# One VectorE instruction with a PSUM operand in place of two, in a graph attention kernel on one core

## The reference

```
alpha = a_src[src] + a_dst[dst] (+ a_edge)        # one value per edge and head
alpha = leaky_relu(alpha, 0.2)
m = segment_max(alpha, dst)
ea = exp(alpha - m[dst])
den = segment_sum(ea, dst)
out = segment_sum(xp[src] * ea[:, :, None], dst)  # later divided by den
```

## Time and profile before

| what | value |
|---|---|
| median of 3 runs | 8124.74 us (8120.78 to 8137.6) |
| time of the profiled execution | 8132.4 us |
| its span | 8130.6 us |
| mean granted clock of TensorE | 0.759 |
| DVE busy | 4106.7 us, 51% of the span |
| PE busy | 4968.6 us, 61% |
| POOL busy | 3807.1 us, 47% |
| the two `weigh` instructions of 110 batches | 2283 ns each in g2, 2283 in g3 |

### The profile page before, as it was taken

How to read it: one execution, slowest core, us unless ns; L and a number is a source line. 1 busy time by engine, 2 the same in 40 slices (tenths; PEclk the granted TensorE clock), 3 DMA queues, 4 the chain that set the end, 5 groups by cost and what they waited for, 6 DMA issues and landing times. The chain is left out here.

```text
span 8130.6 us, 99773 instructions
## 1 busy us (share of the span) xinstructions
PE 4968.6 (61%) x21937; PEld 3493.2 (43%) x21938; DVE 4106.7 (51%) x8878; ACT 3148.1 (39%) x9208; POOL 3807.1 (47%) x3656
## 2 busy tenths in 40 slices
PE   1777777777877875555555355655653355555651
PEld 0555555555655663344443233333332233333331
DVE  2344444444444664222222546666667656666668
ACT  1555555555555323333334233333333333333332
POOL 1233333333333102666666046666664266666663
PEclk7888888888888667777777677777776667777775
DMA  5322222222222102434343133333331233333332
GB/s 197 91 50 49 53 52 49 50 54 50 49 55 49 30 18 86 113 111 114 111 113 104 48 112 108 108 109 107 109 109 44 63 105 106 106 105 105 107 104 71
DMA packets 675121, 685.46 MB, mean 84 GB/s; under 512 B 454519, under 2 KB 542809, under 8 KB 672974
## 3 DMA queue, kind: packets, MB, share of 16 engines
q0 software_dynamic: 171984, 482.58, 20.8%
q1 hardware_dynamic: 492941, 188.51, 9.3%
q10 hardware_dynamic: 10016, 12.59, 0.4%
HBM read 625.13 MB, written 65.79 MB: 85 GB/s over the span
## 5 line engine op out<-in xcount | busy, mean ns | idle before, releaser
L913 POOL DMA_INDIRECT c0rows<-rows,c0idx x880 | 832.3, 946 | 1593.8 <-DVE c0prod L1069 1342.3
L1525 POOL DMA_INDIRECT g3rows<-sender_rows,g3idx x880 | 976.9, 1110 | 617.9 <-issue 232.3
L1525 POOL DMA_INDIRECT g2rows<-sender_rows,g2idx x880 | 975.2, 1108 | 571.5 <-issue 229.8
L721 POOL DMA_INDIRECT g1rows<-rows,g1idx x880 | 831.6, 945 | 687.0 <-issue 243.8
L953 ACT ACTIVATE c0selk<-c0sel,c0sh 128x128 f32<-128x128 f32 x3520 | 1063.0, 392 | 3.1 <-PE c0psA L1022 3.1
L754 PE MATMUL g1psA<-g1rows,g1sel 128*128 128x257 f32 x1760 | 606.8, 519 | 554.6 <-issue 421.2
L1022 PEld LDWEIGHTS c0psA<-c0prod,c0selk 128*128 128x128 f32 x5280 | 829.7, 215 | 67.0
L832 DVE TENSOR_TENSOR acc<-acc,g1psA 128x257 f32 x880 | 372.1, 423 | 949.3 <-issue 554.0
L1019 PE MATMUL c0psA<-c0prod,c0selk 128*128 128x256 f32 x1760 | 658.0, 460 | 298.2 <-DVE acc L1084 283.0
L1022 PE MATMUL c0psA<-c0prod,c0selk 128*128 128x128 f32 x5280 | 820.2, 297 | 0.0
L754 PEld LDWEIGHTS g1psA<-g1rows,g1sel 128*128 128x128 f32 x1760 | 462.5, 271 | 685.3 <-issue 550.0
(11 more groups left out here) (412 smaller groups left out, 7901.8 us busy)
## 6 DMA issues: line engine op xcount, KB each, us to landing
g2bc<-dst_rows SPq DMA_DIRECT2D x55, 512.0 KB
g3bc<-dst_rows SPq DMA_DIRECT2D x55, 512.0 KB
g1f<-in_edge_attr SPq DMA_DIRECT2D x83, 320.0 KB
c0rows<-rows,c0idx POOLq DMA_INDIRECT x880
g1rows<-rows,g1idx POOLq DMA_INDIRECT x880
g2rows<-sender_rows,g2idx POOLq DMA_INDIRECT x880
g3rows<-sender_rows,g3idx POOLq DMA_INDIRECT x880
rbf_steps<-prep_extra ACTq DMA_DIRECT2D x7, 1024.0 KB, 5.7
```

The source lines that it names most:

```text
L721: g.indirect_dma_start(rows[b][:, u, 0:D], None, k.table, bass.IndirectOffsetOnAxis(ap=idx[b][:, u:u + 1], axis=0)).then_inc(r_sem[b], 16)
L913: g.indirect_dma_start(rows[b][:, u, :], None, k.table, bass.IndirectOffsetOnAxis(ap=idx[b][:, u:u + 1], axis=0)).then_inc(g_sem[b], 16)
L1525: g.indirect_dma_start(rows[b][:, u, 0:TW], None, k.sender_rows, bass.IndirectOffsetOnAxis(ap=idx[b][:, u:u + 1], axis=0)).then_inc(gas[b] ...
```

## The change

ScalarE computes the exponential twice: once from PSUM into columns 384 to 511 of the same PSUM bank, then once as before into `rows[b]`. VectorE's product takes the weights from PSUM, broadcast over the 32 channels, and handles all 16 steps in one instruction, which adds 2 to `msg` when it ends. TensorE's transpose of `z` into that bank now also waits until that product of the batch before has ended.

```diff
             def turn(t):
                 pe.wait_ge(S["z"], t + 1)
-                reach(pe, S["w"], t)
+                reach(pe, S["msg"], t * 2)
                 nc.tensor.transpose(psT[:, 0:P], z[:, :, :].rearrange("p h u -> p (h u)"), k.ident[:, :]
                                     ).then_inc(S["zt"], 1)
...
+                nc.scalar.activation(psT[:, 3 * P:4 * P], psT[:, P:2 * P], ACT.Exp)
                 nc.scalar.activation(by, psT[:, P:2 * P].rearrange("p (h u) -> p h u", h=H), ACT.Exp
                                      ).then_inc(S["w"], 1)
                 one_hot(t, 0)
...
             def weigh(t, b, i):
                 v.wait_ge(S["w"], t + 1)
-                for half in range(2):
-                    u = slice(half * (U // 2), (half + 1) * (U // 2))
-                    r = rows[b][:, u, 0:TW].rearrange("p u (h c) -> p u h c", c=HW)
-                    nc.vector.tensor_tensor(r[:, :, :, 0:CH], r[:, :, :, 0:CH],
-                                            r[:, :, :, CH:HW].broadcast_to([P, U // 2, H, CH]), ALU.mult
-                                            ).then_inc(S["msg"], 1)
+                weight = psT[:, 3 * P:4 * P].rearrange("p (h u) -> p u h", h=H)
+                r = rows[b][:, :, 0:TW].rearrange("p u (h c) -> p u h c", c=HW)
+                nc.vector.tensor_tensor(r[:, :, :, 0:CH], r[:, :, :, 0:CH],
+                                        weight.unsqueeze(3).broadcast_to([P, U, H, CH]), ALU.mult).then_inc(S["msg"], 2)
```

## The result

| | median | range | runs |
|---|---|---|---|
| before | 8122.76 us | 8120.01 to 8137.6 | 4 |
| after | 8267.51 us | 8264.44 to 8275.23 | 4 |

The changed kernel takes 1.0181 of the time, 95% interval 1.0169 to 1.0194. That is 145 us more; the profiled executions differ by 137.3 us (8132.4 and 8269.69). This holds for the chip of the first measurement. What the runs show of both follows. Ratios are estimated from all runs of a kernel, so they lie up to 0.0006 beside the quotient of two medians; left out are one run of the kernel before on chip 3 (9144.82 us) and one of late_gather_b on chip 4 (9582.89 us), both over 30% above the rest.

The account below looks back on a forecast made before the run. Each interval was taken as weigh, score, products, gather 0 (7.6 us), then 18.6 us tied to gathers. Delays of 167, 6 and 4 us sum to 177: 8309 profiled, less 7.7, gives 8302 us; range 8175 to 8345.

Parts of the forecast that it names:

- the 18.6 us behind gather 0: From gather 0 to the next weigh: a stretch that stays fixed, so a later gather 0 moves the weigh one for one.
- One instruction: VectorE's weigh: one instruction takes 4.41 us where two halves take 4.48, a gain of 0.07 us.
- The operand in PSUM: VectorE's weigh: reading the factor from PSUM adds nothing, as `rescale` broadcasts from PSUM at the plain product's cost.
- The other end: VectorE's weigh: dear PSUM reads, 0.72 ns an element, +2.9 us a batch; as a rival 8620 us, chance 0.05.
- The second exponential: ScalarE before the weigh: 0.3 to 0.5 us more, costing nothing within 1.9 us of cover, at worst 0.4.
- TensorE's start: Product 0 waits for the whole weigh, 2.13 us later; product 3 and gather 0 move by 1.9 us, to about +9.5.
- The wait in `turn`: TensorE's added wait costs nothing, since it has waited for `msg` of the same batch before product 0.
- How many batches: Batches of g2 and g3 that pay the delay: 102 - 14 = 88, by 1.9 us, 167 us.
- The intervals without gathers: Four intervals bound by VectorE, whose `within` waits for the later transpose: 4 x 1.5 = 6 us.
- the shrinking: Sign of a wrong forecast: the stretch from gather 0 to the next weigh shrinks when gather 0 comes later.
- Gathers beside the weigh: GpSimd: back to 0.95 us if VectorE's two SBUF operands hold them; 2.25 us freed, worth nothing behind product 3's wait.
- The rival: Faster: if GpSimd's own queue set gather 0, 2.25 us off 102 intervals, 230 us, so 7895 us; chance 0.04.

Follow-up runs that it names:

- late_gather_b: Kernel before with gather 0 (and so 1 to 3) waiting for product 5 instead of product 3; 6945.07 us, ratio 0.9998 to before.
- experiment 4: On top of experiment 1, each gather waits for its own step's product, where gathers 0 to 3 waited for product 3; 8398.20 us, ratio 1.0148 to before.
- experiment 1: Changed kernel with the weigh in two halves again, PSUM factor and second exponential kept; 8287.15 us, ratio 1.0009 to the kernel before.
- experiment 2: Kernel before with the weigh merged into one instruction, factor still from SBUF, no second exponential; 8394.90 us, ratio 1.0146 to before.
- experiment 3: Kernel before with the second exponential alone, written to PSUM and read by nobody; 8278.39 us, ratio 1.0004 to before.
- guard_rescale: Kernel before with gather 12 waiting for the semaphore of the rescale at the batch's end instead of product 15's; 6944.99 us, ratio 1.0001 to before.

## Why the prediction held on the first chip, and where it did not

*What bounds the kernel.* On chips 1 and 2 as said: gathers, in a way I couldn't name, set 7 us of each interval. The step that read the 18.6 us behind gather 0 as fixed was too strong. They are twelve gathers and mostly 4.6 to 5.4 us behind the last one (experiment 4). With the guards unchanged the two say the same in most batches, and so the forecast came out right: the trace that it was read from and the result are of the same chip. Carried over to chip 3 it has the wrong sign. What holds the other engines stays open.

*One instruction.* 4.41 forecast, 4.411 measured as the mean of 51. Right.

*The operand in PSUM.* No extra cost: 4.48 for two halves with either factor (experiment 1). The other end, 2.9 us a batch, is out. The Trainium skill (VectorE: DVE Perf Modes, "The TRN2 errata") gives a PSUM source a fixed cost 62 cycles higher. An estimate by it is 0.13 us more for the two halves. The rows don't bear it out: 4.48 both ways, and for one instruction 4.411 from PSUM against 4.416 from SBUF (experiment 2).

*The second exponential.* Nothing, as forecast; shown alone by experiment 3. That the one-hot matrices are ready long before product 0 is true of most batches of the changed kernel. With two halves it is not always so: in 17 of the 51 intervals of g2 in experiment 1 product 0 waits for them and starts 0.2 us late.

*TensorE's start.* Product 0 at +4.55 as forecast; the transpose's pass at +7.34 against +7.3, gather 0 at +9.43 against +9.5. The six passes of the first three products cover 3.00 us, as before, so the clock did not come to their help. Experiments 1 and 2 show that this start, and neither operand nor exponential, is the cause on a chip with holds: undone, the ratio is 1.0009; alone, 1.0146. That it works through gather 0, and not through the late products themselves, is argued from the timelines and not shown: no run with gather 0 late alone fell on a chip with holds. Two things speak for it. In experiment 4 nothing but the gathers' guard was changed against experiment 1, and the batch grew by 1.4 us in g2. And where no holds arise, the late products fit into a batch of 20.4 us: in g2 on chip 3 (21.3 in g3), and in the short batch shown below on chip 1.

*The wait in `turn`.* No row of VectorE or TensorE has it as a wait of its own. Nothing, as forecast.

*How many batches.* This term was mis-sized: 88 batches by 1.9 us, 167 us, where the 102 intervals measure 51 x 1.53 and 51 x 1.10, 134 us. In most intervals the delay is 1.8 as forecast (the one shown: 27.95). What the count left out is every sixth batch. There GpSimd stands 1.8 to 1.9 us behind gather 0, in both kernels, and the profile names no reason. In the kernel before 13 of the 16 such batches take 26.4 to 27.5 us. In the changed kernel they are the short ones, 20.4 to 27.3 us: in most of them the weigh comes while the run of gathers still lasts. The batch after each pays with 28.8 to 35.3. One such pair, GpSimd's rows and then VectorE's:

```profile
5082.31 0.95 POOL L1525 DMA_INDIRECT g2rows<-sender_rows,g2idx  x1 [1.86 <-issue]
...
5107.64 0.95 POOL L1525 DMA_INDIRECT g2rows<-sender_rows,g2idx  x1 [6.73 <-PE g2psA L1551]
```

```profile
5070.47 4.41 DVE L1741 TENSOR_TENSOR g2rows<-g2rows,g2psT 128x4096 f32<-128x4096 f32 x1
...
5090.91 4.41 DVE L1741 TENSOR_TENSOR g2rows<-g2rows,g2psT 128x4096 f32<-128x4096 f32 x1
...
5126.20 4.41 DVE L1741 TENSOR_TENSOR g2rows<-g2rows,g2psT 128x4096 f32<-128x4096 f32 x1
```

The first takes 20.44 us, the second 35.29. So the median gather 0 is 1.8 us later in g2 and 1.9 in g3, with 18.6 us behind it as before. In the mean it is 2.4 and 1.8 us later, and the stretch behind it is 0.9 and 0.7 us shorter. That is the shrinking which the prediction named as a sign of being wrong, and it comes for the most part from these pairs. The intervals without gathers grew by 1.0 and not 1.5.

*Gathers beside the weigh.* That VectorE's two SBUF operands hold them was right, on every chip. The rule of the Trainium skill (SBUF — State Buffer, "Who interferes with whom") has VectorE with two SBUF inputs contend with GpSimd instructions that read SBUF. All these runs agree with it if issuing a gather counts as one of them, which the section doesn't say: 0.95 us with one SBUF input, 1.89 to 5.08 with two. The same section of the Trainium skill says that `tensor_tensor` was not seen to stall a DMA. For these gathers the rows show that it does. That this is "worth nothing" was right only under its own condition, that GpSimd waits for product 3 anyway. The rival named the mechanism and the point from which it decides, GpSimd's own queue setting the gathers, and priced it at 2.25 us an interval, 230 us. On the chips without holds that point is passed. The changed kernel gains 194 us on chip 3, 1.8 us an interval in the mean, since the merging takes some back in g3; with the halves kept the gain is 239 us on chip 4, close to that price. Its chance of 0.04 was worked out from one chip's trace, and that could not show that there are chips on which the holds are absent.

## What to carry to other kernels

When work is handed on in parts, the first part's end is what the next engine starts from: one instruction over everything costs the consumer half the producer's time, here 2.1 us for 0.07 saved. A VectorE product with two SBUF operands may stop GpSimd's gathers for as long as the instruction lasts; a PSUM operand avoids it, and it pays as soon as GpSimd's queue is the bound. An edit that you price at nothing because another wait covers it should be priced without the cover too: here the cover was there on some chips and not on others, and the sign of the change with it.

## What the runs showed of the hardware

- The same program takes 17 to 19% longer on two chips (8122.76 and 8278.74 us) than on three others (6941 to 6946). The durations of single instructions are the same (the weigh 4.41, a gather 0.95). What differs is that on the first two semaphore waits of VectorE and ScalarE, and with them TensorE's work, end late while GpSimd issues a run of gathers. VectorE's adds are then 2.82 us apart instead of 0.64, and GpSimd's own wait for product 15 ends late too: gather 12 starts at 5488.04 in the batch shown, though TensorE's last product began before 5478.80. Of the 1180 us between chips 1 and 3, some 750 lie ahead of the first weigh of g2 (it starts at 4778 us on chip 1, and at 4033 in guard_rescale on chip 3), in other layers that gather too; that these have the same holds is not shown.
- A gather that began beside a weigh with two SBUF operands ended 0.81 to 0.83 us after that instruction and no sooner, in each of the seven kernels here that have such a weigh. It took 1.89 to 2.94 us with two instructions, 4.30 to 5.08 with one, and 0.95 with a PSUM factor.
- A VectorE product of 128 x 4096 with its second factor broadcast from PSUM takes 4.411 us (chip 1); with it broadcast from SBUF 4.416 (chip 2) and 4.417 (chip 5).
- GpSimd stands 1.8 to 1.9 us behind gather 0 of every sixth batch of g2 and g3, before and after the change on chip 1.
